# One matmul over the whole PE array in place of four on 32-column strips, in the mixture, the input mixing and the output projection

## The reference, cut to what matters

```python
mixed = tanh(einsum('bte,he->bth', x, W_in) + b_in + ctx)         # input mixing
h1 = gru(mixed, Wih0, Whh0, ...); h2 = gru(h1, Wih1, Whh1, ...)   # 1024 steps each, batch 2
#   r = sigmoid(xr + hr); z = sigmoid(xz + hz); n = tanh(xn + r * hn); h = (1 - z) * n + z * h
x = x + (gate[:, None, :] * h2 + h2) @ W_out.T + b_out            # output projection
shared = silu(xf @ w1) * (xf @ w3) @ w2                           # 256 -> 512 -> 256
h = gelu(einsum('nc,ech->enh', xf, W1e)); y = einsum('enh,ehc->enc', h, W2e)   # 8 experts
x = x + (shared + combine_of_top_2(y)) / 3
```

## Time and profile before

| | |
|---|---|
| median of 3 runs | 2195.38 us |
| lowest and highest | 2190.18 and 2202.85 us |
| span of the profiled execution | 2185.8 us |
| PE busy | 2068.4 us (95%) |
| DVE busy | 1841.5 us (84%) |
| ACT busy | 1201.4 us (55%) |
| POOL busy | 560.5 us (26%) |
| granted TensorE clock | 0.998 of full, mean |

### The profile page before, as it was taken

One profiled execution on the slowest core, in us unless ns is written; L12 is line 12 of the kernel. 1 busy time (PEld: TensorE's weight loads), 2 busy tenths in 40 slices (PEclk: granted clock), 3 DMA queues, 4 the chain that ended last, 5 costly groups with the idle time before them and its releaser, 6 DMA issues.

```text
span 2185.8 us, 162058 instructions
## 1 busy us (share of the span) xinstructions
PE 2068.4 (95%) x69920; PEld 1485.0 (68%) x69920; DVE 1841.5 (84%) x11225; ACT 1201.4 (55%) x6471; POOL 560.5 (26%) x2542
## 2 busy tenths in 40 slices
PE   6989899999999999999999999999999999999987
PEld 3666666677666776767767676666767676777766
DVE  4888889888888888888888888888888888888874
ACT  2555555555555555555555555555555555555542
POOL 1222232222322223222222222222232222222220
PEclk9999999999999999999999999999999999999999
DMA  5000000000000000000000000000000000000000
GB/s 219 4 4 5 4 5 5 24 5 5 9 5 24 5 5 10 5 24 5 10 5 24 5 5 9 5 24 5 5 10 5 24 5 10 5 21 9 5 16 19
DMA packets 10879, 32.76 MB, mean 15 GB/s; under 512 B 1368, under 2 KB 6832, under 8 KB 9136
## 3 DMA queue, kind: packets, MB, share of 16 engines
q1 hardware_dynamic: 10160, 22.38, 2.8%
HBM read 20.22 MB, written 2.16 MB: 10 GB/s over the span
## 4 chain that ended last, share of the span: by engine, by line
PE 60%; DVE 26%; ACT 10%; issue 3%; DMA 1%; SPq 0%; POOL 0%; DVEq 0%; POOLq 0%
PE bank L333 29%; PE bank L325 17%; PE bank L272 11%; DVE n_first L404 9%; DVE cells L424 7%; ACT factors L472 6%; ACT cells L476 4%; DVE r_pre L395 4%; DVE z_pre L405 3%; PE bank L306 3%; DVE bank L413 1%; DVE n_second L380 0%; DVE x L687 0%; PE bank L657 0%; DVE hid L745 0%
## 5 line engine op out<-in xcount | busy, mean ns | idle before, releaser
L333 PE MATMUL bank<-w_h,cells 128*22 128x128 f32 (+4 forms) x32768 | 1363.4, 281 | 23.6 <-DVE cells L424 13.9
L333 PEld LDWEIGHTS bank<-w_h,cells 128*22 128x22 f32 (+4 forms) x32768 | 853.0, 111 | 130.5 <-DVE cells L424 91.3
L325 PEld LDWEIGHTS bank<-w_h,cells 128*2 128x2 f32 (+15 forms) x28112 | 512.2, 113 | 528.1 <-DVE cells L424 502.8
L517 POOL TENSOR_SCALAR cells<-cells 128x4 f32<-128x4 f32 x2048 | 463.6, 226 | 1525.8 <-DVE cells L424 1524.8
L325 PE MATMUL bank<-w_h,cells 128*2 128x64 f32 (+15 forms) x28112 | 770.1, 225 | 76.3 <-DVE cells L424 55.5
L466 ACT ACTIVATE n_second<-r_pre 128x4 f32<-128x4 f32 x2048 | 426.3, 208 | 508.8 <-DVE r_pre L395 466.3
L472 ACT ACTIVATE factors<-z_pre 128x4 f32<-128x4 f32 x2048 | 429.6, 210 | 436.5 <-DVE z_pre L405 358.8
L404 DVE STREAM_TRANSPOSE n_first<-bank 128x64 f32<-128x64 f32 x2048 | 600.0, 293 | 33.1 <-PE bank L333 23.7
L424 DVE TENSOR_TENSOR_SCAN cells<-factors,cells 128x18 f32<-128x18 f32 x2048 | 397.2, 194 | 241.5 <-ACT cells L476 177.1
L395 DVE STREAM_TRANSPOSE r_pre<-bank 128x64 f32<-128x64 f32 x2048 | 480.6, 235 | 33.3 <-PE bank L325 24.9
L405 DVE STREAM_TRANSPOSE z_pre<-bank 128x64 f32<-128x64 f32 x2048 | 427.4, 209 | 0.0
(11 more groups left out here) (91 smaller groups left out, 558.8 us busy)
## 6 DMA issues: line engine op xcount, KB each, us to landing
c_all<-weights SPq DMA_DIRECT2D x6, 1024.0 KB
x_t<-in_x_t SPq DMA_DIRECT2D x4, 512.0 KB, 7.4
w_1e<-in_w_1e SPq DMA_DIRECT2D x1, 2048.0 KB
w_2e<-in_w_2e SPq DMA_DIRECT2D x1, 2048.0 KB
w_x<-in_w_x SPq DMA_DIRECT2D x2, 768.0 KB, 8.2
w_h<-in_w_h SPq DMA_DIRECT2D x2, 768.0 KB, 9.5
w<-in_w SPq DMA_DIRECT2D x3, 512.0 KB
out_y<-y SPq DMA_DIRECT2D x6, 256.0 KB, 3.5
```

Source lines behind the costliest of these rows:

```text
L325: mm = pe.matmul(r_sums[l][p][32 * g:32 * g + B * (j + 1)], state_tile(l, j, kt), w_h[l][:, kt, g, 2 * U:], start=False, stop=False, tile_ ...
L333: mm = pe.matmul(sums[l][p][32 * g:32 * g + B * (j + 1), 0:width], state_tile(l, j, kt), w_h[l][:, kt, g, 0:width], start=False, stop=Fals ...
L517: pool.tensor_scalar(cell_part(step_rows(l, j), 3), cell_part(step_rows(l, j), 1), 0.5, None, ALU.mult)\
```

## The change

`by_columns` issues one matmul in place of four. The stationary tile is the full 128 columns of `w`, the output all 128 partitions of the bank, the moving operand the same. No order, wait or buffer is changed; the recurrence, its projections and the bias matmuls keep their strips.

```diff
         def by_columns(pe, ps, w, x, start, stop):


-            for g in range(NQ):
-                strip = slice(32 * g, 32 * g + 32)
-                mm = pe.matmul(ps[strip], w[:, strip], x, start=start, stop=stop, tile_position=(0, 32 * g),
-                               skip_group_check=True)
+            mm = pe.matmul(ps, w, x, start=start, stop=stop, skip_group_check=True)
             return mm
```

## The result

| | before | after |
|---|---|---|
| median | 2196.65 us (4 runs) | 2300.34 us (4 runs) |
| lowest to highest | 2190.18 to 2202.85 | 2299.64 to 2303.24 |
| span of the profiled execution | 2185.8 us | 2298.0 us |

The changed kernel is slower by 4.8%: the ratio is 1.0482, with a 95% interval of 1.046 to 1.0505. The prediction was 2305 us in a range of 2197 to 2350.

A forecast was written before the change was run, and what follows sets the result against it. The recurrence's chain was taken to bound ordinary slots, PE those with two products. Losses of 63, 16 and 34 us, 113 together, took the span from 2185.8 to 2299; plus 9.6 gave 2308, rounded to 2305, range 2197 to 2350.

The forecast's parts named there:

- What bounds the kernel: Ordinary slots: the recurrence's chain, so one product is free; slots with two products are all PE, 2.21 us.
- Emptying, both ways: PE between strips and whole array: the array empties on entering and leaving, 0.045 to 0.09 us each; chance 0.56.
- The load: A product's 128-column weight loads: the first bare, 0.11 us at full clock; the second hidden under the first pass.
- X: Time added on PE by each product between recurs: 0.24 to 0.33 us, taken as 0.28.
- From X to the slot: Ordinary one-product slots lose (0.28 - 0.05) / 2 = 0.115 us, slots with r not first 0.22, two-product slots 0.56.
- Fewer instructions: PE's waits put down to issue: 12 fewer records a product save 1.5 us by their share, left out.
- the 9.6 us: Excess of the median of the runs over the profiled span, added to the forecast span of 2299 to give 2308.
- the sum of 113: Loss over all slots beside the recurrence: 63, 16 and 34 us in three stretches.
- No drain: PE's changes of shape: the late load has another cause, X below 0.05, 2195 to 2203 us; chance 0.17.
- one-sided drain: PE's changes of shape: strips to whole costs only 0.03, X 0.08 to 0.14, 2213 to 2240 us; chance 0.14.
- the faster rival: PE's loads: if their 23 us of issue waits come from fetching instructions, up to 23 us go, 2172; chance 0.05.

The follow-up runs named there:

- the tiny matmuls: Kernel before, on strips, plus one whole-array matmul of 2 zero columns ahead of each mixture and output-projection product: 1.1151, about +253 us.
- the strip control: Kernel before plus four strip matmuls of 2 zero columns ahead of each mixture and output-projection product, no change of shape: 1.0638, about +140 us.
- the split and doubled transfers: Kernel before, on strips, with the c_all transfer issued as four transfers of two experts each: 0.9973; or issued twice with the same data: 1.0059.

## Why the prediction was right, point by point

**What bounds the kernel.** Right. A product hid completely in an ordinary slot: slots with and without one had medians of 1.987 and 1.984 us.

**Emptying, both ways.** Right, and at the upper end. I had one row, of one direction, at the half clock, with 0.09 us, and left open whether it scales with the clock. It doesn't: 0.09 on entering and on leaving at 2.4 GHz, and by the modelled ends of the records 0.09 at 1.2 GHz too. (That those first loads ran at the half clock the profile doesn't record, since its clock starts at 12 us; the changed kernel's first products show it, with starts 0.427 us apart up to 11.5 us and 0.216 from 11.9 on.) The choice for two directions over one was an argument from the overlap of the strips; the 0.09 us before the load of line 270 shows it. The rule of the Trainium skill ("TensorEngine Tiling (Array Packing)", Key Properties: changing the mode drains, changing the tile doesn't) agrees with the runs: 0.27 to 0.45 us whenever tiles of another width come between, 0.084 for the same loads on the same strips.

**The load.** Right: 0.104 bare once, from 379 against 431 ns in the mean of two, for an estimate of 0.11 made by halving the half-clock row; hidden under the first pass the second time.

**X.** Taken as 0.28, measured 0.31, within 0.24 to 0.33.

**From X to the slot.** Right: half of X in ordinary slots. With 0.31 the rule gives (0.31 - 0.05) / 2 = 0.13, the medians grew by 0.143. Slots where r isn't first grew by 0.232 (0.22 forecast), slots with two products of 256 tokens by 0.615 in the median (0.56, or 0.62 at the true X).

**The terms that were mis-sized.** Fewer instructions: put at 1.5 us and left out. At the true X the sum is about 125 to 130 us, and 112 came between the two profiled executions. The difference is in the first stretch: by medians it should have grown by some 405 x 0.143 + 65 x 0.232 = 73 us between slots 128 and 792, and it grew by 56. The 17 us are irregular slots of the kernel before that the changed one doesn't have (405 x (0.054 - 0.011), what the mean stands above the median before and after); the waits for instructions above 0.4 us alone fell by 11.5.

The other term is the 9.6 us that I added for what lies around the span. The four executions of the changed kernel are 1.8 us longer than their spans, and its median is 2.3 above the profiled span. The rest of the 9.6 was no constant: with as much around its span of 2185.8, the profiled execution of the kernel before was shorter than any of its four runs, which spread over 12.7 us where those of the changed kernel spread over 3.6. Between medians the change cost 103.7 us, 9 less than the sum of 113. So X too small stood against two terms wrong the other way, the waits for instructions and the 9.6, and 3 us went in rounding; that the predicted time lies within 0.2% of the measured one is partly luck.

**The rivals.** No drain and one-sided drain are excluded by the 0.09 us before the load in both directions and by the tiny matmuls. Of the faster rival the mechanism was there: the waits do come from fetching PE's instructions, and most of them went, with 6% fewer records and 5% more time for them. It was not enough to matter beside 130 us.

**What stays open.** That PE's waits for issue grow with its number of records is shown by the strip control (from 23 to 100 us at recur's loads for 13248 more), and that they are waits for its instructions by the landing of the packets. That the longest come from packets queuing behind the transfer of c_all is shown by the late packets and by the split and doubled transfers. What limits how close together the other packets come isn't shown, nor why moving the products' waits onto instructions of their own took 9 us off. In the changed kernel fewer records and longer slots go together, and no run here separates them. What made the clock fall in the kernel with the tiny whole matmuls wasn't followed up.

## What to carry to other kernels

Where some matmuls sit on column strips, a matmul of another tile width between them costs about 0.3 us in this kernel, nearly all of it independent of its size: keep one shape through a loop whose steps wait for one another, or put all work of the other shape behind one change. Before costing an addition to a "95% busy" engine, find which slots are full: here the same X cost half of itself in one kind of slot and all of itself in another. And on an engine fed with 64 records a microsecond, count records as well as time: here it waited for instructions where a slot asked for 72. A forecast that starts from one profiled execution should ask where that execution lies among the others.

## What the runs showed of the hardware that I had not expected

- The strips of PE run on independently: with one strip at work on a product of 256 columns, the other three took the next matmuls 0.19 us after its start (1642.70 and 1642.89).
- 9% more matmul and load records on PE raised its waits for issue at the recurrence's loads from 23 to 100 us. All 460 such waits over 0.4 us beside the recurrence, in fourteen profiles, end 1.17 to 1.73 us behind the landing of a 16 KB instruction packet, and one packet comes for every 255 of PE's records.
- Behind two of the three waits above 2 us for instructions the granted clock fell to 1.2 GHz for a slot (0.51 at 941 us and 0.52 at 1470 us of the kernel before).
- The emptying of the array takes 0.09 us at 2.4 GHz (0.093 to 0.095 at 1408 of 1421 changes) and, by the modelled ends of the records, as much at 1.2 GHz.
